# Embedding with row choice and gather batch by batch, and routing with transposes in two sets of banks and logits directly behind their encoder products

## The reference

```
# embedding with tuned rows: 50257 x 192 table, 256 rows replaced
out  = base_weight[input_ids]
rows = id2row[input_ids]              # -1 where the id is not in tune_ids
h    = where(rows >= 0, train_weight[max(rows, 0)], out)
...
h = h + attention(layernorm(h))       # 12 heads of 16
# switch feed-forward, 8 experts of width 64
x_enc      = xt @ enc_w + enc_b       # 192 -> 64
route_prob = softmax(x_enc @ sw_w + sw_b)     # 64 -> 8
routes     = argmax(route_prob)
h = h + max(route_prob) * expert[routes](xt)
...
h = h + test_time_training_attention(layernorm(h))
h = h + soft_mixture_of_32_experts(layernorm(h))
```

## Time and profile before

| | |
|---|---|
| median of 3 runs | 1359.38 us (1358.72 to 1360.54) |
| profiled execution | 1361.78 us, span 1360.0 us |
| TensorE busy | 1239.5 us, 91% of the span |
| VectorE busy | 924.1 us, 68% |
| ScalarE busy | 728.3 us, 54% |
| GpSimd busy | 391.5 us, 29% |
| mean granted TensorE clock | 0.961 |

### The profile page before, as it was taken

How to read it: one execution, slowest core, us unless ns; L and a number is a source line. 1 busy time by engine, 2 the same in 40 slices (tenths; PEclk the granted TensorE clock), 3 DMA queues, 4 the chain that set the end, 5 groups by cost and what they waited for, 6 DMA issues and landing times. The chain is left out here.

```text
span 1360.0 us, 29202 instructions
## 1 busy us (share of the span) xinstructions
PE 1239.5 (91%) x11299; PEld 858.0 (63%) x11299; DVE 924.1 (68%) x2294; ACT 728.3 (54%) x1529; POOL 391.5 (29%) x445
## 2 busy tenths in 40 slices
PE   4889999889879999899999988999976899899998
PEld 3432333345647777677777767788864455588888
DVE  6578888422489998899888878888874999300001
ACT  1436555523134553788888864788874344433310
POOL 6500000100058897655666640000000334200000
PEclk9979999959879999999999998999987999999999
DMA  3442211110034456634343541121103200177711
GB/s 99 111 121 61 58 48 48 40 48 1 1 102 158 154 179 194 194 95 125 104 136 99 151 119 53 54 69 43 47 1 128 96 1 0 58 264 280 283 62 47
DMA packets 103127, 133.71 MB, mean 98 GB/s; under 512 B 25358, under 2 KB 88573, under 8 KB 98797
## 3 DMA queue, kind: packets, MB, share of 16 engines
q1 hardware_dynamic: 100396, 129.73, 31.0%
q0 software_dynamic: 1536, 1.59, 0.5%
q10 hardware_dynamic: 1056, 0.52, 0.1%
HBM read 89.06 MB, written 37.88 MB: 93 GB/s over the span
## 5 line engine op out<-in xcount | busy, mean ns | idle before, releaser
L1817 POOL TENSOR_SCALAR r_grD<-gr 32x192 f32<-32x192 f32 x192 | 101.5, 529 | 94.1 <-PE bank L1548 55.2
L700 ACT ACTIVATE PT<-bank 128x1024 f32<-128x1024 f32 x96 | 94.2, 1022 | 58.9 <-PE bank L580 58.3
L641 DVE TENSOR_REDUCE mx<-bank 128x1 f32<-128x512 f32 x176 | 109.9, 681 | 11.7 <-PE bank L563 11.4
L2579 DVE TENSOR_TENSOR eo_all<-bank,m_b2s 128x768 f32<-128x768 f32 x8 | 7.7, 958 | 138.5 <-PE bank L2540 138.5
L1548 PE MATMUL bank<-r_grD,ek 128*128 128x256 f32 x384 | 100.0, 396 | 0.0
L2571 ACT ACTIVATE x_g<-bank,m_b1s 128x128 f32<-128x128 f32 x192 | 51.4, 400 | 75.7 <-PE bank L2522 75.7
L1375 POOL TENSOR_TENSOR rope_c<-cy,p_rope 128x512 f32<-128x512 f32 x48 | 70.9, 1497 | 19.1 <-DVE cy L1223 19.1
L2453 POOL TENSOR_SCALAR m_xs<-m_xs 128x256 f32<-128x256 f32 x4 | 2.5, 630 | 250.2 <-DVE m_xs L2344 250.2
L1548 PEld LDWEIGHTS bank<-r_grD,ek 128*128 128x128 f32 x384 | 67.7, 189 | 9.3
L1761 ACT ACTIVATE r_t<-r_xh,r_cd 128x64 f32<-128x64 f32 x192 | 70.0, 427 | 0.6
L1539 PEld LDWEIGHTS bank<-gr,r_A 128*128 128x128 f32 x384 | 47.7, 191 | 33.0 <-DVE gr L1711 31.9
(11 more groups left out here) (381 smaller groups left out, 3207.3 us busy)
## 6 DMA issues: line engine op xcount, KB each, us to landing
wb<-in_m_w SPq DMA_DIRECT2D x32, 1152.0 KB, 6.3
ek<-k_d SPq DMA_DIRECT2D x32, 384.0 KB
k_d<-t_late SPq DMA_DIRECT2D x46, 256.0 KB, 2.8
tgt<-c_d SPq DMA_DIRECT2D x33, 196.0 KB
c_d<-t_late SPq DMA_DIRECT2D x32, 196.0 KB, 3.0
rope_s<-cy SPq DMA_DIRECT2D x48, 128.0 KB, 2.1
g_d<-gr SPq DMA_DIRECT2D x32, 192.0 KB
o_G<-g_d SPq DMA_DIRECT2D x32, 192.0 KB, 2.9
```

The lines of the kernel that those rows point to most:

```text
L641: v.tensor_reduce(mx[u % 2][:, j // 4, j % 4:j % 4 + 1], slot(f"A{u}.{j}"), AX.X, ALU.max).then_inc(*dve.did(f"max{u}.{j}"))
L700: a.activation(PT[kt % 2][:, 2 * hp:2 * hp + 2, :], STB[s % 2][:, :, :], ACT.Exp, scale=DH ** -0.5)\
L1817: last = g_.tensor_scalar(grD[g][rr, :, b, :], b3(gr[j % RING][rr, cols(g)]), 0.0, None, ALU.bypass)
```

## The change

In `embed`:
- VectorE no longer waits for the tuned ids before it handles the ids; the two loads have semaphores of their own. The two memsets of the mask rows of `Q` and `K` move from the front to behind the second batch of `tuned_rows`.
- `hit`, `best`, `none` and `tuned_u` are computed batch by batch. Batches 0 to 2 come before the norms of `phi`, batch 3 behind the first layer norm and the scaling of `phi`. GpSimd waits for the `tuned_u` of a batch alone, and writes its own mask values behind the `train` of batch 0.
- The scaling of `phi` moves from in front of the first layer norm to behind it, and TensorE's wait for it from in front of the first transposes to behind them.
- TensorE issues four `fill` products between `spread` and the first transposes.
- SyncE writes `phi` out before it copies the mask rows, and not behind.

In the routing of `switch_ffn`:
- The transposes of odd batches go to `ps[4:6]`, those of even batches to `ps[0:2]`, so that `turn(b)` waits for `xT{b-2}` and not for `xT{b-1}`.
- The encoder product of batch b comes in front of `turn(b + 1)`, and `logits(b)` directly behind that.
- Four `fill` products and not seven stand in front of `turn(0)`, and one behind it.
- ScalarE takes `root(1)` before `out_of(0)`.

```diff
@@ embed, VectorE
-                v.memset(Q[0][MASK_ROW:MASK_ROW + 1, :, :], NEG)
-                v.memset(K[0][MASK_ROW:MAX_ROW + 2, :, :], 1.0).then_inc(cleared, 1)
-                v.wait_ge(loaded, 32)
+                v.wait_ge(ids_in, 16)
                 v.tensor_copy(ids16f[:, :], ids16[:, :]).then_inc(*dve.did("idsf"))
...
+                v.wait_ge(tune_in, 16)
                 v.tensor_copy(tune_f[:, :], tune_i[:, :])
...
-                for t in range(TILES):
-                    last = v.scalar_tensor_tensor(hit[:, t, :], tune_f[:, :], ids_f[:, t:t + 1], rank_f[:, :],
-                                                  ALU.is_equal, ALU.mult)
+                def tuned_rows(b):
+                    of = slice(b * TB, (b + 1) * TB)
+                    for t in range(b * TB, (b + 1) * TB):
+                        last = v.scalar_tensor_tensor(hit[:, t, :], tune_f[:, :], ids_f[:, t:t + 1], rank_f[:, :],
+                                                      ALU.is_equal, ALU.mult)
...
+                tuned_rows(0)
+                tuned_rows(1)
+                v.memset(Q[0][MASK_ROW:MASK_ROW + 1, :, :], NEG)
+                v.memset(K[0][MASK_ROW:MAX_ROW + 2, :, :], 1.0).then_inc(cleared, 1)
+                tuned_rows(2)
...
                 layer_norm(0)
+                scaled_slots()
+                tuned_rows(3)
@@ embed, TensorE
                 last.then_inc(spread, 1)
+                fill(t_, VB[1], ident, 4)
+
...
-                    if b == 0:
-                        t_.wait_ge(normed, 2)
...
                     t_.wait_ge(*act.at(f"xT1.{b}"))
+                    if b == 0:
+                        t_.wait_ge(normed, 2)
@@ embed, GpSimd
-                    g.wait_ge(*dve.at("tuned"))
+                    g.wait_ge(*dve.at(f"tuned.{b}"))
...
                     train(b)
+                    if b == 0:
+                        g.wait_ge(cleared, 1)
+                        g.memset(Q[0][MASK_ROW:MASK_ROW + 1, :, 0:1], 0.0)
+                        g.memset(K[0][MASK_ROW:MASK_ROW + 1, :, 1:N], 0.0).then_inc(cleared, 1)
@@ switch_ffn, TensorE
-                    if b:
-                        t_.wait_ge(*act.at(f"xT{b - 1}"))
+                    if b >= 2:
+                        t_.wait_ge(*act.at(f"xT{b - 2}"))
...
-                fill(t_, ps[7], ident, 7)
+                fill(t_, ps[7], ident, 4)
                 turn(0)
+                fill(t_, ps[7], ident, 1)
...
                 for b in SB:
-                    if b + 1 < B:
-                        turn(b + 1)
                     t_.wait_ge(*act.at(f"xT{b}"))
...
                     last.then_inc(*pe.did(f"enc{b}"))
-                    if b:
-                        logits(b - 1)
-                logits(B - 1)
+                    if b + 1 < B:
+                        turn(b + 1)
+                    logits(b)
@@ switch_ffn, ScalarE
                 root(0)
+                root(1)
                 out_of(0)
-                root(1)
                 root(2)
```

More of the change, by code:

```diff
@@ L104, in embed @@
         firsts = lambda after: [f"A{j}" for j in range(*AT_PE[after])]
-        dve = Steps(sem("e_dve"), ["eps", "idsf", "ids", "rank", "hits", "best", "none", "tuned"]
-                    + [f"{n}.0" for n in ("stats", "aggr", "rstd", "xn")]
+        dve = Steps(sem("e_dve"), ["eps", "idsf", "ids", "rank"] + [f"{n}.{b}" for b in range(3) for n in ("hits", "best", "none", "tuned")]
+                    + [f"{n}.0" for n in ("stats", "aggr", "rstd", "xn")] + [f"{n}.3" for n in ("hits", "best", "none", "tuned")]
                     + [s for b in SB for s in (peaks(0, 3) if b + 1 == B else []) + [f"rest0.{b}"] + (peaks(3, 5) if b + 1 == B else []) + [f"rest1.{b}"]
@@ L130, in _ @@
                 sp.dma_start(M["blk"][:, :], ins["c_blk"]).then_inc(consts, 16)
+                for k in range(KC):
+                    sp.wait_ge(normed, k + 1)
+                    sp.dma_start(M["phin_d"][k * DC:(k + 1) * DC, :], phi[:, k, :]).then_inc(phi_out, 16)
                 sp.wait_ge(cleared, 2)
@@ L214, in _ @@
                 v.memset(eps[:, :], LN_EPS).then_inc(*dve.did("eps"))
-                v.memset(Q[0][MASK_ROW:MASK_ROW + 1, :, :], NEG)
-                v.memset(K[0][MASK_ROW:MAX_ROW + 2, :, :], 1.0).then_inc(cleared, 1)
-                v.wait_ge(loaded, 32)
+                v.wait_ge(ids_in, 16)
                 v.tensor_copy(ids16f[:, :], ids16[:, :]).then_inc(*dve.did("idsf"))
                 v.wait_ge(turned, 1)
-                v.tensor_copy(ids_f[:, :], IDS[:, 0:TILES])
-                v.tensor_copy(ids_u[:, :], IDS[:, 0:TILES]).then_inc(*dve.did("ids"))
+                v.tensor_copy(ids_u[:, :], IDS[:, 0:TILES])
+                v.tensor_copy(ids_f[:, :], IDS[:, 0:TILES]).then_inc(*dve.did("ids"))
+                v.wait_ge(tune_in, 16)
                 v.tensor_copy(tune_f[:, :], tune_i[:, :])
@@ L225, in _ @@
                 v.wait_ge(*dve.at("rank"))
-                for t in range(TILES):
-                    last = v.scalar_tensor_tensor(hit[:, t, :], tune_f[:, :], ids_f[:, t:t + 1], rank_f[:, :],
-                                                  ALU.is_equal, ALU.mult)
[L229 to L237, removed]
+                def tuned_rows(b):
[3 more added lines that the diff above has]
+                                                      ALU.is_equal, ALU.mult)
+                    last.then_inc(*dve.did(f"hits.{b}"))
+                    v.wait_ge(*dve.at(f"hits.{b}"))
+                    v.tensor_reduce(best[:, of], hit[:, of, :], AX.X, ALU.max).then_inc(*dve.did(f"best.{b}"))
+                    v.wait_ge(*dve.at(f"best.{b}"))
+                    v.tensor_scalar(none[:, of], best[:, of], 0.0, 70000.0, ALU.is_equal, ALU.mult)\
+                        .then_inc(*dve.did(f"none.{b}"))
+                    v.wait_ge(*dve.at(f"none.{b}"))
+                    v.scalar_tensor_tensor(tuned_u[:, of], best[:, of], 1.0, none[:, of], ALU.subtract, ALU.add)\
+                        .then_inc(*dve.did(f"tuned.{b}"))
+                tuned_rows(0)
[3 more added lines that the diff above has]
+                tuned_rows(2)
                 v.wait_ge(rooted, 1)
@@ L244, in _, with scaled_slots @@
                 v.tensor_scalar(unit[:, :], unit[:, :], scale[:, 0:1], None, ALU.mult).then_inc(united, 1)
[L245 to L250, removed]
+                def scaled_slots():
+                    v.wait_ge(spread, 1)
+                    for k in range(KC):
+                        for hf in range(2):
+                            cols = slice(hf * SL // 2, (hf + 1) * SL // 2)
+                            last = v.tensor_tensor(phi[:, k, cols], phi[:, k, cols], QK[hf][0:DC, :], ALU.mult)
+                        last.then_inc(normed, 1)
                 def layer_norm(b):
@@ L784, in switch_ffn @@
                           if k >= YLAG and (k - YLAG) % CE == CE - 1 else [])])
-        act = Steps(sem("f_act_s"), ["std0", "xT0", "std1", "std2", "xe0", "xT1", "std3", "xe1", "xT2", "xe2", "xT3", "xe3",
+        act = Steps(sem("f_act_s"), ["std0", "std1", "xT0", "std2", "xe0", "xT1", "std3", "xe1", "xT2", "xe2", "xT3", "xe3",
                                      "ex"] + [f"hotT{b}" for b in SB] + [f"gelu{k}" for k in K] + ["nroot"])
         lined = sem("f_lined")
-        pe = Steps(sem("f_pe"), ["T0"] + [n for b in SB for n in ([f"T{b + 1}"] if b + 1 < B else [])
-                                          + [f"enc{b}"] + ([f"lg{b - 1}"] if b else [])]
-                   + ["lg3", "h0", "h1"] + [f"hotT{b}" for b in SB]
+        pe = Steps(sem("f_pe"), ["T0"] + [n for b in SB for n in [f"enc{b}"] + ([f"T{b + 1}"] if b + 1 < B else []) + [f"lg{b}"]]
+                   + ["h0", "h1"] + [f"hotT{b}" for b in SB]
                    + [n for k in range(len(K) + YLAG) for n in
```

18 lines of the change are left out of this document (7 added, 11 removed).

## The result

The changed kernel takes 1337.07 us (1335.81 to 1341.67, 4 runs), the kernel before, on the same chip, 1359.96 us (1358.72 to 1361.06, 4 runs): ratio 0.9844, 95% interval 0.982 to 0.9868. So it is faster by 1.6%, 22.9 us between the medians; 1336.5 was forecast. The profiled execution is the slowest of the four: 1341.67 us, span 1339.9, mean granted clock 0.972.

The account below looks back on a forecast made before the run. It took the routing to be bound by TensorE at 1.2 GHz and the embedding by its ring and late gathers. 6.4 + 17.3 = 23.7 from 1361.78 gives 1338.1, the median 2.4 lower: 1335.7, rounded to 1336.5; range 1331 to 1353.

Parts of the forecast that it names:

- The routing: Routing of `switch_ffn`: TensorE's clock stays at 2.4 GHz, `hot` is transposed at 290.1 and not 307.41, 17.3 us gained.
- Its steps: Routing: encoder product of batch 0 at 271.1, 4.0 us a batch, logits end at 286.7, `hot` transposed at 290.1.
- delays nobody else: Routing, ScalarE: `root(1)` moved ahead holds up no other work, as VectorE has `xn1` at 272.5, before TensorE wants it.
- The embedding: Embedding stage: 4.4 us from layer norm 3 plus 2.0 from the clock in batch 3, 6.4 gained, bounds 1 and 8.
- most of the fill runs at the lower clock: Embedding, TensorE: eight fill records take 3.6 us at the high clock, 6.9 at half; the fill ends at about 31.2.
- the ring: Embedding: products, splitting, layer norm, transposes; 10.8 us a batch puts layer norm 3 at 60.4, not 64.80, 4.4 gained.
- The loads of the `K` rows: End of the embedding: rows SyncE loads for the first scores are next late, costing up to 0.8 of the 4.4 us.
- The stretch without dense products: Embedding, in front of batch 3's products: shrinks from 4.61 to between 2.8 and 3.6 us, so the clock may stay.
- its term of 2.0: Embedding, batch 3: with the clock kept, eight records cost 0.45 each, up to 3.4 us gained; 2.0 taken.
- First gather: Embedding, GpSimd: gathers start from about 4.4 us, 3.5 to 4 earlier than before.
- A routing at 1.2 GHz: Rival, 22%: the routing falls to the low clock all the same, logits end 2 to 2.8 us earlier only; 1350.6 us.
- the embedding gives nothing: Rival, 10%: late fill, held gathers or row loads cancel the embedding's gain; only the routing's 17.3 remains, 1342.1 us.

Follow-up runs that it names:

- routing_only: Kernel before with the changed `switch_ffn` and the old `embed`: ratio 0.9893 (0.9863 to 0.9924), 1345.12 us; routing 26.70 us.
- fill_only: Kernel before with three fill products added behind the first transposes of the routing: ratio 0.9974 (0.9953 to 0.9995), routing 39.79 us.
- old_order: Changed kernel with only TensorE's old order put back in the routing: ratio 0.9856 (0.9816 to 0.9896), routing 34.70 us.
- old_filled: old_order with more fill products where TensorE waits in the routing: ratio 0.9907 (0.9884 to 0.9929), routing 30.93 us.
- the second set: old_filled, embed_nofill, embed_fill_only and tail_fill, compared with the kernel before on another chip, where the kernel before takes 1365.83 us.
- embed_only: Kernel before with the changed `embed` and the old `switch_ffn`: ratio 0.9952 (0.9926 to 0.9978), 1353.67 us; routing 41.27 us.
- after_again: The changed kernel word for word, run again beside three edits: 1337.05 us (6 runs), ratio 0.9831 (0.9798 to 0.9863), routing 28.40 us.
- embed_fill_only: Kernel before with only the four fill products behind `spread` in `embed` added: ratio 0.9952 (0.9931 to 0.9973), routing 40.61 us.
- embed_nofill: Changed kernel without the four fill products in `embed`: ratio 0.9855 (0.9834 to 0.9877).
- tail_fill: Changed kernel with two fill products added behind the transposes of batch 3 in `embed`: ratio 0.9843 (0.9827 to 0.9859).

## Why the prediction was right, point by point

**The routing** was forecast to give 17.3. Measured: 15.2 in the profiled execution, 16.9 where the clock holds in `hidden` (43.64 - 26.70). Against the 40.6 that the old routing took in another profile it would be 12.2 to 13.9, and routing_only's ratio of 0.9893 is 14.6 us (10 to 19) of the median; so 17.3, taken from one profile in which the clock fell early, lies at the upper end. Its steps, counted from the stage's first `fill`, forecast first: encoder product of batch 0 at 7.3, 7.28; period 4.0, 4.1; logits over at 22.9, 23.3; `hot` at 26.3, 28.40 or 26.70. The mechanism, a clock that stays up because no long stretch without products is left, is shown by profiles of one execution each: fill_only and old_order lose it at idle stretches of 1.89 and 2.40 us, and old_filled, the same order with these filled, keeps it. The stretches between encoder products hold only transposes and thin logits, and eight profiles show 1.00 from the first encoder product to the last logits. The Trainium skill's rule that the prediction weighed, that transposes do not count as work for the clock as products do ("TensorE: Matmul & The Clock Gate", Part 4), did not decide it. It is not refuted by that: these stretches are 2.2 us long, shorter than the 2.80 that kept the clock before.

What was wrong in it is small: the second set of banks gives 0.0, which I had said, but `root(1)` costs 0.5 where I counted a gain ("delays nobody else" left out `xT0`), and the forecast did not have the clock fall in `hidden`.

**The embedding** came out at 6.5 (89.80 to 83.32), forecast 6.4, by other terms, and that agreement is luck. `spread` began at 22.17, not 21.3. The step that failed is "most of the fill runs at the lower clock": the eight records took 3.88 us, 0.49 each (3.60 to 4.79 us in the other profiles). I had read the fill as the first dense work behind a pause, as batch 0 is in the earlier trace rows, and had not seen that it stands directly behind `spread`, 3.73 us of products. So the fill ended at 29.5, not 31.2, and the products began at 31.18, not 33.8. From there the ring went as forecast: layer norms at 36.16, 46.78 and 57.51, steps of 10.6 and 10.7, no wait for a gather. That is 7.3 for the ring, not 4.4.

The tail took back what the ring gave. From the transposes of batch 3 to the attention it is 22.4 us, 21.6 before: 0.8 lost where 2.0 had been forecast as a gain. The loads of the `K` rows, priced at up to 0.8, are waited for during 1.95 us and start the products 1.2 later behind their transposes (3.41 us, 2.22 before). The stretch without dense products shrank from 4.61 to 3.80 us, just above the 2.8 to 3.6 of the forecast, and the clock was at 0.50 at its end, from 63.97 on. The idea of that step holds in the other profiles, where a stretch of up to 3.61 us keeps the clock; its term of 2.0 did not come in this one. A kept clock is worth 3.1 us (3.4 was its upper end). Two errors of 2.9 and 2.8 us cancelled.

How much the changed embedding gives in general is less certain than 6.5. The attention begins at 86.13, 89.27 and 89.80 in the three profiles of the old one outside the second set, and at 82.95 to 84.11 in the seven of the new; embed_only's ratio allows 3 to 10 us.

First gather: forecast 4.4, measured 5.66; the cast of `ids` took 1.56 beside the 0.64 of the earlier trace rows. Layer norm 0 did not wait for it. The hold of a gather beside VectorE's work came back once, 2.65 us at 40.15, and twice in after_again (2.68 at 40.13 and at 50.77), where layer norm 3 then waited.

**The rivals.** A routing at 1.2 GHz did not come in any of eight profiles. That the embedding gives nothing is excluded by embed_only.

## What to carry to other kernels

Before adding filler work to keep a clock up, look for the gap behind it: here three fills in the old order gained 0.3% in the routing, since the clock fell at the next wait of 1.89 us, and in the embedding fills left batch 0 as slow as it was, with 4.0 us between them and the first product. Fills in every wait kept the clock (30.93 us), but an order in which each engine's next instruction is already free did so in 26.70. Read a clock forecast from the whole row of work that will stand together after the change, the instructions that were short of a gap before included. An independent step moved ahead on an engine can still wait for its own input and hold up the one behind it: check when its input is due, not only what it reads.

## What the runs showed of the hardware that was not expected

- The granted clock falls at other places from one execution to the next with nearly the same instructions: in `hidden` in three of eight profiles, in one from 255 to 265 us, in front of the routing (granted clock 0.59), and in the old routing behind an idle stretch of 3.06 us (before) but not behind one of 3.05 (embed_fill_only). Once down, it came back inside the old routing in old_order (1.00 from 272 us) and embed_fill_only (1.00 from 281.7), and not in 30 us of it before (0.50). The changed kernel spread over 9 us in one set (1333.53 to 1342.52), and the intervals of that set's ratios are 0.3% to either side; six runs do not tell differences of 2 or 3 us apart.
- In all four profiles of the second set, on the other chip, TensorE, ScalarE and VectorE stalled in the embedding between 30 and 50 us; 7.63 us in front of the products of batch 1 in embed_nofill, put down to "issue", 4.09 for a late copy in tail_fill, and least in embed_fill_only (2.26 where before shows 1.15). None of the ten others shows it at that place, and before was 4 to 7 us slower on that chip. No cause was tried; it stays open.
- The same products stand beside a bf16 score at either level: four records of 512 columns in 1.88 us (embed_fill_only) and in 3.62 (changed kernel), behind waits of 1.93 and 1.95 us for the same rows of `K`. The length of the idle stretch in front does not tell them apart, the granted clock does (1.00 and 0.50).
